# Softmax outputs as three rounded products, split transposes and exchanged banks in a fused two-layer cross-attention kernel

## The reference

```python
# layer 0 (x: 512 tokens, ctx: 64 rows, idx: one context index for each token)
q = rmsnorm(x) @ Wq0.T;  k, v = rmsnorm(ctx) @ Wk0.T, rmsnorm(ctx) @ Wv0.T
scores = q . k / sqrt(hd)                  # per head
w = where(|key - idx| <= 1, relu(scores)**2, 0)
x1 = x + ((w / max(sum(w), 1e-6)) . v) @ Wo0.T
# layer 1
q1 = gelu(x1 @ Wq1 + bq); k1 = gelu(ctx @ Wk1 + bk); v1 = gelu(ctx @ Wv1 + bv)
a = softmax(q1 . k1)                       # 512 x 64, one head
z = a @ v1 @ Wf + bf + x1
out = layernorm(z) * gamma + beta
```

## Time and profile before

| | |
|---|---|
| median of 3 runs | 343.87 us (343.45 to 344.19) |
| profiled execution, its own time | 343.76 us |
| its span in the profile | 342.0 us |
| PE busy | 324.4 us, 95% of the span |
| DVE busy | 287.9 us, 84% |
| ACT busy | 250.8 us, 73% |
| POOL busy | 231.9 us, 68% |

### The profile page before, as it was taken

How to read it: one execution, slowest core, us unless ns; L and a number is a source line. 1 busy time by engine, 2 the same in 40 slices (tenths; PEclk the granted TensorE clock), 3 DMA queues, 4 the chain that set the end, 5 groups by cost and what they waited for, 6 DMA issues and landing times.

```text
span 342.0 us, 5710 instructions
## 1 busy us (share of the span) xinstructions
PE 324.4 (95%) x1914; PEld 238.7 (70%) x1914; DVE 287.9 (84%) x456; ACT 250.8 (73%) x598; POOL 231.9 (68%) x233
## 2 busy tenths in 40 slices
PE   8999999999999999999999999999999999989980
PEld 3675678868686767776768687776768686857750
DVE  2789598888888888898988888898888888889766
ACT  4898524587878787969696969697887878785752
POOL 4416170246979696969788787878797969665414
PEclk9999999999999999999999999999999999999996
DMA  6987635934253433425261616162624242110103
GB/s 234 389 249 201 196 109 128 252 83 140 76 184 93 167 110 141 137 105 172 71 207 61 216 61 213 66 202 76 183 94 161 103 150 91 52 61 0 63 0 123
DMA packets 30268, 46.34 MB, mean 136 GB/s; under 512 B 2400, under 2 KB 16736, under 8 KB 30240
## 3 DMA queue, kind: packets, MB, share of 16 engines
q1 hardware_dynamic: 27264, 37.86, 36.0%
q0 software_dynamic: 2016, 7.34, 5.3%
q10 hardware_dynamic: 960, 0.79, 0.7%
HBM read 25.14 MB, written 8.39 MB: 98 GB/s over the span
## 4 chain that ended last, share of the span: by engine, by line
PE 76%; DVE 18%; issue 3%; ACT 2%; DVEq 0%
PE ps L532 12%; PE ps L533 12%; PE ps L534 12%; PE ps L583 7%; PE ps L577 6%; DVE qkp L1339 5%; PE ps L668 4%; PE ps L785 4%; PE ps L776 4%; PE ps L703 4%; PE ps L617 2%; PE ps L564 2%; DVE kv L1257 2%; PE ps L673 1%; PE ps L517 1%
## 5 line engine op out<-in xcount | busy, mean ns | idle before, releaser
L1293 DVE TENSOR_TENSOR qkp<-ps,bufs 128x1024 f32<-128x1024 f32 x48 | 56.0, 1219 | 9.3 <-ACT bufs L1035 8.0
L443 POOL TENSOR_TENSOR bufs<-bufs,lng_twice 128x1024 f32<-128x1024 f32 x14 | 33.7, 2408 | 27.2 <-ACT bufs L1074 25.1
L432 POOL TENSOR_TENSOR qkp<-qkp 128x1024 f32<-128x1024 f32 x15 | 35.9, 2396 | 21.6 <-DVE qkp L1304 21.6
L389 POOL TENSOR_TENSOR x_lo<-x_ring,x_hi 128x1024 fp32r<-128x1024 f32 x16 | 38.2, 2387 | 7.0 <-ACT x_hi L1031 7.0
L1112 ACT ACTIVATE xp_hi<-bufs 128x512 fp32r<-128x512 f32 x28 | 17.7, 634 | 31.9 <-DVE bufs L1381 31.9
L1304 DVE TENSOR_TENSOR qkp<-ps,wn 128x1024 f32<-128x1024 f32 x31 | 37.6, 1215 | 3.8 <-PE ps L583 3.7
L448 POOL TENSOR_TENSOR bufs<-bufs,lnb_row 128x1024 f32<-128x1024 f32 x14 | 33.5, 2395 | 0.1
L1035 ACT ACTIVATE bufs<-ps 128x512 f32<-128x512 f32 x32 | 19.2, 602 | 14.4 <-PE ps L534 14.4
L532 PE MATMUL ps<-x_hi,wh_q 128*128 128x512 f32 x64 | 26.7, 417 | 0.0
L1042 ACT ACTIVATE bufs<-bufs 128x256 f32<-128x256 f32 x64 | 25.7, 407 | 0.0
L1074 ACT ACTIVATE bufs<-ps,nbias,half_rstd 128x256 f32<-128x256 f32 x52 | 25.2, 566 | 0.3
(11 more groups left out here) (257 smaller groups left out, 920.2 us busy)
## 6 DMA issues: line engine op xcount, KB each, us to landing
x_ring<-xT SPq DMA_DIRECT2D x16, 512.0 KB, 3.4
bufs<-x SPq DMA_DIRECT2D x16, 512.0 KB, 5.0
out<-bufs POOLq DMA_DIRECT2D x14, 512.0 KB, 3.3
idx_ring<-idx SPq DMA_DIRECT2D x16, 256.0 KB, 4.1
wkv_lo<-kv SPq DMA_DIRECT2D x32, 126.0 KB
kvs<-kv SPq DMA_DIRECT2D x30, 126.0 KB
vfd<-bufs SPq DMA_DIRECT2D x8, 256.0 KB, 4.7
qkp<-ctxT SPq DMA_DIRECT2D x2, 512.0 KB, 6.7
```

What stands on the lines that cost most here:

```text
L389: G.tensor_tensor(x_lo[:, :, :], x_ring[:, e % RING, :, :], f32_view(x_hi[:, :, :]), ALU.subtract).then_inc(xl_ready, 2)
L432: G.tensor_tensor(att[:, 1, :, :], att[:, 0, :, :], att[:, 1, :, :], ALU.add).then_inc(pair_ready, 1)
L443: G.tensor_tensor(zo, zn, lng_twice[:, :].unsqueeze(1).broadcast_to([P, TT, D]), ALU.mult).then_inc(zg_ready, 1)
L1293: V.tensor_tensor(qk[:, s, :, :], ps[:, bank0:bank0 + 2, :], q0, ALU.mult).then_inc(qk_ready, 1)
```

## The change

Four edits.

1. The softmax output of the 13 sequences `n` = 0 to 12 is made of three float32r products: `eT_hi` with `vf_hi`, `eT_hi` with `vf_lo`, `eT_lo` with `vf_hi`, four matmuls each. ACT writes `eT_hi` where it wrote `eT`, and rounds one sequence's values to `vf_hi`; DVE makes the remainders `eT_lo` and `vf_lo`. The outputs of sequences 13, 14 and 15 stay as they were.
2. The eight transposes of x' are split: four stand before the two transposes of the scores, four behind.
3. From the second sequence on, the picked keys UP go to banks 0 and 1 and the picked keys DOWN to banks 6 and 7, and the waits go with the banks.
4. The transposes of x', which write banks 6 and 7, wait for the multiplication of the keys DOWN (`qk_ready` 3a + 3) in place of that of the keys UP (3a + 2).

On TensorE:

```diff
             def up_keys(a):
                 pe.wait_ge(kvs_in[a % 2], 64 * (a // 2 + 1))
-                picked_keys(a, UP, 6)
+                picked_keys(a, UP, 6 if a == 0 else 0)
...
                     pe.wait_ge(eT_ready, n + 1)
-                    if n == 0:
-                        pe.wait_ge(vfd_in, 16 * 8)
-                    for u in range(2):
-                        for h in range(2):
-                            half = slice(h * K, (h + 1) * K)
-                            i = mm(out_rows(2 * h + u), eT[half, u, :], vfd[half, n, :], start=False, stop=True, skip_group_check=True)
+                    pe.wait_ge(eTl_ready, n + 1)
+                    pe.wait_ge(vfl_ready, n + 1)
+                    for weights, values in ((eT_hi, vf_hi), (eT_hi, vf_lo), (eT_lo, vf_hi)):
+                        for u in range(2):
+                            for h in range(2):
+                                half = slice(h * K, (h + 1) * K)
+                                i = mm(out_rows(2 * h + u), weights[half, u, :], values[half, :], start=False,
+                                       stop=weights is eT_lo, skip_group_check=True)
                     i.then_inc(z_mm, 1)
...
+                def back(tiles):
+                    for j in tiles:
+                        for c in range(DC):
+                            mm(out_rows(j, c * P, P), xpT[:, c, j * P:(j + 1) * P], ident,
+                               is_transpose=True, start=(j % 2 == 0 and c == 0), stop=False, skip_group_check=True)
...
                 if a is not None:
-                    if n is not None:
-                        pe.wait_ge(zn_ready, 2 * n + 2)
-                    if f == 0:
-                        pe.wait_ge(k1_copied, 4)
+                    pe.wait_ge(att_ready, 3 * f + 2)
                     up_keys(a)
...
                 if a is not None:
-                    pe.wait_ge(att_ready, 3 * f + 2)
-                    picked_keys(a, DOWN, 0)
+                    if n is not None:
+                        pe.wait_ge(zn_ready, 2 * n + 2)
+                    if f == 0:
+                        pe.wait_ge(k1_copied, 4)
+                    picked_keys(a, DOWN, 6)
...
                     if a is not None:
-                        pe.wait_ge(qk_ready, 3 * a + 2)
+                        pe.wait_ge(qk_ready, 3 * a + 3)
                     else:
                         pe.wait_ge(zn_ready, 2 * n + 2)
-                    for j in range(TT):
-                        for c in range(DC):
-                            mm(out_rows(j, c * P, P), xpT[:, c, j * P:(j + 1) * P], ident,
-                               is_transpose=True, start=(j % 2 == 0 and c == 0), stop=False, skip_group_check=True)
+                    back((0, 1))
                     pe.wait_ge(scT_cp, b + 1)
                     for u in range(2):
                         i = nc.tensor.transpose(ps[:, 4, (2 + u) * P:(3 + u) * P], scT[:, u * P:(u + 1) * P], ident)
                     i.then_inc(sc_mm, 1)
+                    back((2, 3))
```

On ScalarE, in `step`:

```diff
+                def round_values(m):
+                    if m == 0:
+                        act.wait_ge(vfd_in, 16 * 8)
+                    else:
+                        act.wait_ge(z_mm, m)
+                    A(vf_hi[:, :], vfd[:, m, :], ACT.Copy).then_inc(vfh_ready, 1)
...
+                if n == 0:
+                    round_values(0)
                 if n is not None:
                     act.wait_ge(eT_mm, n + 1)
-                    A(eT[:, :, :].rearrange("p a t -> p (a t)"), ps[:, 4, 2 * P:4 * P], ACT.Copy).then_inc(eT_ready, 1)
+                    A(eT_hi[:, :, :].rearrange("p a t -> p (a t)"), ps[:, 4, 2 * P:4 * P], ACT.Copy).then_inc(eT_ready, 1)
...
                     square_x(a)
+                if n is not None and n + 1 < OLD - 1:
+                    round_values(n + 1)
```

On VectorE, in `step`:

```diff
+                def values_remainder(m):
+                    dve.wait_ge(vfh_ready, m + 1)
+                    V.tensor_tensor(vf_lo[:, :], vfd[:, m, :], f32_view(vf_hi[:, :]), ALU.subtract).then_inc(vfl_ready, 1)
...
+                if n == 0:
+                    values_remainder(0)
+                if n is not None:
+                    dve.wait_ge(eT_ready, n + 1)
+                    if n > 0:
+                        dve.wait_ge(z_mm, n)
+                    V.tensor_tensor(eT_lo[:, :, :].rearrange("p a t -> p (a t)"), ps[:, 4, 2 * P:4 * P],
+                                    f32_view(eT_hi[:, :, :]).rearrange("p a t -> p (a t)"), ALU.subtract).then_inc(eTl_ready, 1)
...
                     attend(f, 1, DOWN, 0, att_flat(1))
+                if n is not None and n + 1 < OLD - 1:
+                    values_remainder(n + 1)
...
-                    multiply_keys(a, UP, 6)
-                    multiply_keys(a, DOWN, 0)
+                    multiply_keys(a, UP, 0)
+                    multiply_keys(a, DOWN, 6)
```

More of the change, by code:

```diff
@@ L93, in xattn_pair @@
         eT = sb("eT", [P, 2, P])
+        eT_hi = sb("eT_hi", [P, 2, P], f32r)
+        eT_lo = sb("eT_lo", [P, 2, P], f32r)
+        vf_hi = sb("vf_hi", [P, D], f32r)
+        vf_lo = sb("vf_lo", [P, D], f32r)
         stats = sb("stats", [P, TT, 6])
@@ L160, in xattn_pair @@
         twice_ready = sem("twice_ready")
+        eTl_ready, vfh_ready, vfl_ready = map(sem, ("eTl_ready", "vfh_ready", "vfl_ready"))
         pair_ready, last_pair = sem("pair_ready"), sem("last_pair")
```

## The result

| | before | after |
|---|---|---|
| median (lowest to highest) | 343.66 us (343.3 to 344.19, 4 runs) | 347.01 us (346.52 to 348.33, 4 runs) |
| profiled execution, its span | 343.76, 342.0 | 348.33, 346.5 |
| starts of the attention-sum transposes | 17.88 us apart | 18.17 us apart |

The ratio is 1.0102, with a 95% interval of 1.0071 to 1.0134: the change made the kernel 1.0% slower, 3.4 us, where 3.1 us less was forecast. 13 steps times 0.29 us are 3.8 us, so the loss is one of each step.

What follows compares the result with a forecast made beforehand. It took TensorE, busy 17.64 of 17.86 us, to stall once a step behind VectorE. 13 x 0.25 plus 0.20 less 0.36 gave 3.1 us off 343.76, so 340.7, or 340.8 as median; range 339.4 to 341.6, chance 0.58.

Steps and rivals of the forecast that it cites:

- The split transposes: TensorE around the x' transposes: score transposes 0.32 us earlier, 0.12 of new stall, so line 668 starts 0.19 us earlier.
- The softmax output: TensorE at line 703: twelve matmuls as six side-by-side pairs take 0.92 us in place of 1.06, saving 0.14.
- The rival that priced a slower result: Softmax output: halves do not run side by side, output 1.53 to 1.63 us, total 348.5 to 350 us; chance 0.14.
- The price of `eT_lo`: VectorE between 1351 and 1357, without cover: 0.36 us to the next start, 0.42 to its end.
- Three rings: Slowest closed chain sets the period: ScalarE's 17.59, TensorE's 17.53, VectorE's 17.53 us; taken as 17.61, 0.25 less than before.
- VectorE binds: Rival: VectorE's ring, through `eT_lo`, `vf_lo` or a handover, sets 17.68 to 17.76 us, total 341.7 to 342.7; chance 0.16.
- The exchanged banks: Picked keys UP and DOWN: the exchange costs and brings nothing; keys UP's wait ends some 0.1 us before TensorE needs it.
- The sum: Whole kernel: 13 steps at 0.25 us, plus 0.20 in the first step, less 0.36 once: 3.1 us saved.
- the signs named as wrong: Output of 1.5 us; repeated wait at keys UP or x' transposes; maxima starting 0.3 us before table load ends or later.

Runs made afterwards that it cites:

- the fastest kernel: Changed kernel with denominators in PSUM, ScalarE's query copy between the normalising's halves and GpSimd's pair ahead of its scalings: 340.28 us, ratio 0.9892.
- the kernel with the mended clamp: Changed kernel with only the denominators' tile moved from SBUF to a free part of PSUM bank 0: 342.19 us, ratio 0.9978.

## Why the prediction was wrong

- **The split transposes** were right: the stall at line 668 gone, 0.20 us a step gained for 0.19 predicted.
- **The softmax output** was right: 0.90 us for 0.92, and upper and lower halves run side by side. The rival that priced a slower result was wrong in its mechanism: the time ended on its side for another reason, and 347.0 us is inside none of the stated ranges.
- **The price of `eT_lo`** was right in itself (0.33 to the next start, 0.41 to its end, for 0.36 and 0.42). What failed is the next line of that step: the weights, statistics and weighings "wait behind `eT_lo`" at their old prices. The clamp behind it was left at 0.22 and measured 0.62. This is the step that failed: an operation that is moved keeps its price only if its neighbours on other engines don't change, and I didn't look at GpSimd beside it. Once held, the clamp closes a ring through GpSimd's queue (18.17) that my three rings don't have.
- **Three rings** failed too: there is a fourth, from VectorE's statistics over GpSimd's factors to the normalising and the query copy. I took VectorE's ring from the statistics to its own 1381 and ScalarE's stretch from the picked values to the score copy as a fixed 10.99 us, so a later statistic moved neither. That stretch measured 11.55 in the changed kernel (167.31 to 178.86), 11.15 with the denominators in PSUM and 10.99 in the fastest kernel. With the clamp mended the fourth ring closes at 17.77; with half of the normalising taken out of it, the period is 17.61. My 17.61 was thus 0.56 too low, 0.40 for the held clamp and 0.16 for this ring. The rival "VectorE binds" named the right place, `eT_lo`, and its 341.7 to 342.7 hold the kernel with the mended clamp (342.19), but by luck: what is left there is not VectorE's ring as summed.
- **The exchanged banks** cost and bring nothing in the period: right, 17.76 and 17.77.
- **The sum** over 13 steps is nearly right: the clamp is held in 11 of them, so 11 times 0.40 and 13 times 0.16 are 6.5 us, and 340.8 plus 6.5 is 347.3, against 347.0.
- Of the signs named as wrong, the repeated wait was there, at the keys UP (582, which wait for the weighing 1326) and, larger, at `queries1(1)` (537, 13 times, 5.8 us), which I hadn't named; the transposes of x' wait as long as before. In the step shown the keys UP start at 174.44, 0.33 us behind the matmul before them in place of 0.23, so this one costs TensorE 0.10; without the exchange the period was the same, so it isn't what decides.

```profile
PEld ps L582 <- DVE qkp L1326: 4.2, 11, 0.4
```

## What to carry to other kernels

When an operation is put into a queue, list what runs on the other engines beside each operation that it pushes back, above all VectorE operations with two SBUF inputs against GpSimd's instructions and its transfer issues: 0.33 us of new work (`eT_lo` to the next start) became 0.73 here, with 0.40 of it held. Move a small tile to PSUM, put the new operation behind the sensitive one, or let another queue issue the transfer; each of the three took the hold away. And follow every engine's short operations when rings are summed: nine short operations, from 169.62 to 172.70, on an engine that is 66% busy stood on both rings that decided. When an operation ends with another engine's instruction whenever it starts, a new ring is closed, through that engine's queue.

## What the runs showed of the hardware

- A VectorE operation with two SBUF inputs is held while GpSimd issues a transfer: 0.62 in place of 0.22 us, ending 0.07 to 0.09 us behind the issue; with one input in PSUM it takes 0.22 at the same lag. The Trainium skill (SBUF — State Buffer, SBUF: two separate sides) describes a pair of SBUF ports shared by VectorE and GpSimd as an exclusive lock, held for the whole instruction, in which a VectorE operation with two SBUF inputs takes part only against a GpSimd operation that reads SBUF. The traces agree on the two inputs, and show the issue of a transfer on the other side, which that section doesn't name. They differ in time: clamps that started 0.10 to 0.23 us into the issue weren't held (0.22 to 0.25 us), from 0.27 us on they were, where by the page the one that "starts first gets the pair" and all of them would be held. Between 0.23 and 0.27 nothing was measured. GpSimd's computing instructions show both cases: the clamp at 92.44 in the kernel before took 0.36 us and ended 0.08 behind GpSimd's addition (448, with its inputs in SBUF), but with the transfers issued by SyncE 11 clamps started 0.60 to 0.63 us into the comparison (`onehot`, 1.6 us, from SBUF) and took 0.22. So not every GpSimd instruction holds the clamp for all of its recorded time, and what decides it stays open.
- It goes the other way as well. GpSimd's `nbias`, 4 elements a partition, takes 0.20 us alone and 0.60 in most steps of the changed kernel, while VectorE subtracts with two SBUF inputs (`xp_lo`, from 171.96, the first of two 0.69 us long; `nbias` from 172.10 to 172.70); before, it took 0.73 in the median. Where it is held, it ends 0.05 to 0.06 us behind the subtraction. In the medians of all kernels here it took 0.43 to 0.74; no run took this away, so what it costs isn't shown.
- Two float32r matmuls with weights in the upper and the lower 64 rows run side by side although each loads 128 columns of its own: twelve in 0.90 us, where the prediction had 1.49 or more if they didn't.
